# Engine orders written out by hand for a conditioned residual kernel: no loops, halved units, Newton step in PSUM, three buffers for xm and z

## What is computed

```
dg, db, ug, ub = cond @ down_gamma, cond @ down_beta, cond @ up_gamma, cond @ up_beta
down = x @ (down_project * dg + db)        # 256 -> 64, per batch
up   = relu(down) @ (up_project * ug + ub) # 64 -> 256, per batch
x2   = x + (up + x)
styles = cond @ (affine_w / sqrt(128)).T + affine_b
dcoefs = rsqrt(sum((weight * styles)**2, axis=2) + 1e-08)
y    = clip((x2 * styles) @ weight.T * dcoefs + bias, -256, 256)
out  = x2 + y
```

## Time and profile before

| | |
|---|---|
| median of three runs | 96.34 us (96.22 to 96.43) |
| span of the profiled execution, first to last instruction | 93.1 us |
| around the span (96.34 less 93.1) | 3.2 us |
| busy TensorE, VectorE, ScalarE, GpSimd | 79.1, 69.7, 56.8, 56.4 us |
| mean granted TensorE clock | 0.951 |
| moved by DMA | 9.40 MB |

### The profile page before, as it was taken

The page is one execution under the profiler, slowest core; times in us unless marked ns, Lnnn a source line. Parts: engine busy times, 40 slices in busy tenths (PEclk is TensorE's granted clock), DMA queues, the critical chain, the costliest instruction groups (busy, mean ns, idle before and its releaser), DMA issues.

```text
span 93.1 us, 1465 instructions
## 1 busy us (share of the span) xinstructions
PE 79.1 (85%) x408; PEld 49.3 (53%) x408; DVE 69.7 (75%) x113; ACT 56.8 (61%) x125; POOL 56.4 (61%) x42
## 2 busy tenths in 40 slices
PE   3985999999489937999999999999999959969340
PEld 3943497659264623356746665584665634534230
DVE  1002055579999999989997989999799999959900
ACT  6052539493920076274499389929956997993440
POOL 5900222118994997068579656857984799897000
PEclk9999589999999997599999999999999999999995
DMA  1999405160520006000057140050006000601566
GB/s 14 300 317 320 134 0 175 58 199 26 142 83 0 0 13 212 0 4 4 7 178 273 59 166 0 0 196 29 0 0 225 0 0 0 225 4 50 175 233 218
DMA packets 9861, 9.40 MB, mean 101 GB/s; under 512 B 1020, under 2 KB 9792, under 8 KB 9856
## 3 DMA queue, kind: packets, MB, share of 16 engines
q1 hardware_dynamic: 9104, 8.75, 29.0%
q10 hardware_dynamic: 576, 0.33, 1.2%
q0 software_dynamic: 176, 0.26, 1.0%
...
## 4 chain that ended last, share of the span: by engine, by line
PE 50%; DVE 23%; issue 10%; ACT 6%; DMA 5%; POOL 2%; ACTq 1%; DVEq 0%; POOLq 0%
PE ps_y L728 19%; PE ps_down L697 12%; DMA vec_rows<-in_L_cond_bias_dram 5%; ACT ps_y L290 5%; PE ps_io L664 5%; PE ps_io L739 4%; PE ps_up L711 3%; PE ps_y L697 2%; PE ps_up L712 2%; DVE ps_up L426 2%; DVE x L433 2%; DVE dm_t L386 2%; DVE z L474 2%; DVE act_hl L420 1%; DVE z L481 1%
## 5 line engine op out<-in xcount | busy, mean ns | idle before, releaser
L728 PE MATMUL ps_y<-xm,wT 128*128 128x512 f32 x56 | 27.2, 630 | 3.2 <-DVE z L474 2.1
L616 POOL TENSOR_TENSOR x<-x,off_sc 128x1024 f32 (+2 forms) x8 | 16.7, 2090 | 8.2 <-DVE x L433 8.2
L290 ACT ACTIVATE ps_y<-ps_y,vec_cols,demod 128x64 f32<-128x64 f32 x64 | 19.4, 404 | 3.2 <-PE ps_y L728 3.2
L608 POOL TENSOR_TENSOR off_sc<-act_sum,up_tab 128x1024 f32<-128x1024 f32 (+1 forms) x8 | 14.4, 1800 | 8.5 <-ACT act_sum L257 8.5
L728 PEld LDWEIGHTS ps_y<-xm,wT 128*128 128x128 f32 x56 | 10.7, 200 | 15.6 <-issue 10.6
L627 POOL TENSOR_TENSOR xm<-x,style 128x1024 f32 (+2 forms) x8 | 14.2, 1771 | 1.2 <-POOL x L616 0.8
L257 ACT ACTIVATE act_sum<-ps_sum 128x512 f32<-128x512 f32 x8 | 4.8, 598 | 13.9 <-DVE demod L398 7.0
L426 DVE TENSOR_TENSOR ps_up<-ps_up,up_tab 128x1024 f32<-128x1024 f32 x8 | 9.8, 1226 | 1.4 <-PE ps_sum L713 1.2
L433 DVE TENSOR_TENSOR x<-ps_up,x 128x1024 f32<-128x1024 f32 (+1 forms) x8 | 9.8, 1221 | 0.7
L697 PE MATMUL ps_down<-xT,dp_sb 128*64 128x256 f32 x56 | 8.2, 415 | 1.6 <-DVE act_hl L420 1.6
L261 ACT ACTIVATE out_nat<-ps_io 128x1024 f32 (+1 forms) x7 | 7.4, 1055 | 2.9 <-PE ps_io L739 2.9
...
## 6 DMA issues: line engine op xcount, KB each, us to landing
x_nat<-in_x_dram SPq DMA_DIRECT2D x7, 512.0 KB, 3.6
out_dram<-out_nat SPq DMA_DIRECT2D x7, 512.0 KB, 2.9
x_nat<-in_x_dram SPq DMA_DIRECT2D x2, 256.0 KB, 3.0
out_dram<-out_nat SPq DMA_DIRECT2D x2, 256.0 KB, 2.3
w_sb<-in_L_cond_weight_dram SPq DMA_DIRECT2D x1, 256.0 KB, 6.9
...
```

What stands on the lines that cost most here:

```text
L290: last = act.activation(tokens, tokens, ACT.Identity, bias=vec_cols[:, DC + c:DC + c + 1], scale=demod[:, c, bass.ds(t.n * TB + b, 1)])
L608: pool.tensor_tensor(by_batch(off_sc[:, 0:chunks]), sums, per_batch(up_tab[:, 1, 0:chunks, bass.ds(t.n * TB, TB)]), ALU.mult).then_inc(off ...
L616: pool.tensor_tensor(x2[:, t.n, 0:chunks], x2[:, t.n, 0:chunks], off_sc[:, 0:chunks], ALU.add).then_inc(x2_ready, 1)
L728: last = pe.matmul(y_bank(t, o), wT[:, c, o * P:(o + 1) * P], xm[:, t.parity, c], start=(i == 0), stop=(i == DC - 1))
```

## The change

Every engine's program is now a flat list. What moves in it:

- Start: `cond` is loaded from ACT's queue instead of SP's, so `down_project` and tile 1 follow tile 0 on SP directly. PE does `down(0)` ahead of the transposes of `affine_w` and of the two vectors; on POOL's queue the vectors are loaded ahead of `affine_w`. The down tables are made in one DVE copy instead of four, from `ps_up`. ACT makes the squares of the style and of the weight; POOL did.
- The tile kept in SBUF is `hT`, the plain transposed x, one buffer a tile. The second copy (`double`) is gone: x2 is kept halved. The up tables are times 0.5, the style table times 2, `demod` times 0.5, the cap is 128, and `evacuate_out` multiplies by 2.
- `x_nat` has a buffer a tile, `xm` and `z` have three, `act_sum` two. 
- Newton: the root, its argument and the product are in `ps_y[:, 0]`; only the reciprocal and `demod` are in SBUF. The step is done in one piece on DVE, ahead of `scale_down(2)`, and PE waits for it before `linear(0, 0)`, since it lies in the bank that this product writes.
- `transpose_out` comes later relative to `transpose_in` and `linear`; `linear` is at places cut between its two chunks.
- Tiles 5 and 6 are treated like all others. POOL does both chunks to the end. The last tile is cut by tokens, not features: `end_linear(part)` makes both output chunks for half of the tokens in `ps_y[:, part]`, and DVE does scale, caps and `finish` for a half (`end_scale`, `end_cap`, `end_finish`). ACT has no part in its demodulation.

```diff
-        x_nat = sb("x_nat", [P, 2, TJ, D])
-        xT = sb("xT", [P, 2, DC, T])
+        x_nat = sb("x_nat", [P, TILES, TJ, D])
+        hT = sb("hT", [P, TILES, DC, T])
-        act_sum = sb("act_sum", [P, T])
+        act_sum = sb("act_sum", [P, 2, T])
-        x2 = sb("x2", [P, TILES, DC, T])
-        xm = sb("xm", [P, 2, DC, T])
-        z = sb("z", [P, 2, DC, T])
+        xm = sb("xm", [P, 3, DC, T])
+        z = sb("z", [P, 3, DC, T])
...
+        def norm_part(i):
+            return ps_y[:, 0, i * DC * B:(i + 1) * DC * B]
+        norm_sum, norm_q, norm_root, norm_u = (norm_part(i) for i in range(4))
...
-            sp.dma_start(cond_sb[:], cond).then_inc(cond_in, 16)
...
+            act.dma_start(cond_sb[:], cond).then_inc(cond_in, 16)
...
-            def double(t):
-                act.activation(x2[:, t.n].rearrange("p c t -> p (c t)"), ps_io[:], ACT.Copy,
-                               scale=2.0).then_inc(x_doubled, 1)
...
+            def newton_step():
+                dve.wait_ge(root_done, 1)
+                dve.reciprocal(dm_r[:], norm_root).then_inc(newton, 1)
+                dve.wait_ge(newton, 1)
+                dve.tensor_tensor(norm_u, norm_q, dm_r[:], ALU.mult).then_inc(newton, 1)
+                dve.wait_ge(newton, 2)
+                dve.tensor_tensor(norm_u, norm_u, dm_r[:], ALU.mult).then_inc(newton, 1)
+                dve.wait_ge(newton, 3)
+                dve.tensor_scalar(norm_u, norm_u, -0.5, 1.5, ALU.mult, ALU.add).then_inc(newton, 1)
+                dve.wait_ge(newton, 4)
+                dve.scalar_tensor_tensor(out=demod[:].rearrange("p c b -> p (c b)"), in0=norm_u, scalar=0.5,
+                                         in1=dm_r[:], op0=ALU.mult, op1=ALU.mult).then_inc(newton, 1)
+                dve.wait_ge(newton, 5)
...
+            def end_scale(part):
+                dve.wait_ge(end_y_ps, part + 1)
+                first = LAST * TB + part * HB
+                tokens = ps_y[:, part].rearrange("p (c b s) -> p c b s", c=DC, s=S)
+                dve.tensor_tensor(tokens, tokens, per_batch(demod[:, :, first:first + HB]),
+                                  ALU.mult).then_inc(end_scaled, 1)
...
+            def end_linear(part):
+                pe.wait_ge(xm_ready, TILES)
+                pe.wait_ge(z_ready[part], LAST)
+                for o in range(DC):
+                    for c in range(DC):
+                        last = pe.matmul(ps_y[:, part, o * HT:(o + 1) * HT], wT[:, c, o * P:(o + 1) * P],
+                                         xm[:, LAST % 3, c, halves(part)], start=(c == 0), stop=(c == DC - 1))
+                last.then_inc(end_y_ps, 1)
...
+            up(1)
+            pe.wait_ge(newton, 5)
+            linear(0, 0)
+            pe.wait_ge(lo_ready, 2)
+            linear(0, 1)
+            down(3)
...
```

More of the change, by code:

```diff
@@ L12 @@
 P = 128
-Tile = namedtuple("Tile", "n parity half")
 CLAMP = 256.0
@@ L338, in _ @@
[L338 to L351 removed]
+            evacuate_sum(0)
@@ new lines, in _ @@
+            scale_up(2)
+            finish(0, 1)
+            add_up(2)
+            relu_low(3)
+            demodulate(1)
+            cap(1, 0)
+            finish(1, 0)
+            scale_down(4)
+            sum_down(4)
+            scale_up(3)
+            relu_low(4)
+            cap(1, 1)
+            add_up(3)
+            finish(1, 1)
+            scale_down(5)
+            cap(2, 0)
+            sum_down(5)
+            finish(2, 0)
+            scale_up(4)
+            demodulate(2)
@@ new lines, in _ @@
+            relu_low(5)
+            cap(2, 1)
+            add_up(4)
+            finish(2, 1)
+            scale_down(6)
+            cap(3, 0)
+            sum_down(6)
+            finish(3, 0)
+            scale_up(5)
+            demodulate(3)
+            relu_low(6)
+            cap(3, 1)
+            add_up(5)
+            finish(3, 1)
+            scale_down(7)
+            cap(4, 0)
+            sum_down(7)
+            finish(4, 0)
+            scale_up(6)
+            demodulate(4)
@@ new lines, in _ @@
+            add_up(6)
+            relu_low(7)
+            cap(4, 1)
+            finish(4, 1)
+            scale_up(7)
+            cap(5, 0)
+            finish(5, 0)
+            demodulate(5)
+            add_up(7)
+            cap(5, 1)
+            finish(5, 1)
+            cap(6, 0)
+            finish(6, 0)
+            demodulate(6)
+            cap(6, 1)
+            finish(6, 1)
+            for part in range(2):
+                end_scale(part)
+                end_cap(part)
+                end_finish(part)
```

816 lines of the change are left out of this document (337 added, 479 removed).

## The result

The changed kernel takes 88.46 us (median of four runs, 88.26 to 89.51) against 96.31 us (96.22 to 96.43) for the kernel before: a ratio of 0.9198, 95% interval 0.914 to 0.9256, 7.9 us less. The profiled execution took 88.29 us, with a span of 86.1 us and 2.2 us around it.

The account below looks back on a forecast made before the run. TensorE was taken as the bound in the middle, VectorE a near second. Span 93.1, less 6.5 gained, plus 1.3 given back, gives 87.9; with 3.2 around it, 91.2 us forecast, range 89.3 to 94.4.

Parts of the forecast that it names:

- 6.5 gained: From the beginning to the results of up(3): these come at 38.6 instead of 45.10 us.
- 1.3 given back: At the end of the kernel, where less work is shared: 1.3 us of the gain lost again.
- The start: Up to the results of up(0): through at 16.2 instead of 19.2, 3.0 us earlier, 1.7 of it the clock.
- one dip stays: Rival, chance 0.14: the start's DMA leaves TensorE half idle, one clock dip costs 1.7 us, time 92.9.
- Newton: Tile 0's second half: four small steps at 0.21 to 0.28 us each, 1.2 us instead of 4.4.
- of the 3.5 beyond the first stage 1.7 is again the clock: From up(0)'s results to up(3)'s: 3.5 us gained, 1.7 of it from the clock dip being gone.
- the sum over VectorE: Middle and end: VectorE's work from 16.2, 64.6 us, plus 1.7 of waits, gives 82.5 and a span of 86.9.
- TensorE's walk: Middle and end, walked through TensorE: waits of 0.5 to 0.9 us at three products, giving a span of 88.6.
- gains nothing by itself: ACT's saved copy, 1.02 us a tile: claimed to gain nothing by itself, since ACT waits.
- Newton as long as before: Rival, chance 0.06: Newton in PSUM is no shorter and now gates linear(0, 0), time 94.1 us.
- the late ring: Rival, chance 0.14: the add_up, POOL, linear, ACT, cap ring stalls VectorE 0.4 us in six tiles, time 93.6.
- the slower one: Rival, chance 0.09: TensorE's short waits in every tile bring repeated clock dips, 1.7 us each; four give 98.0.

Follow-up runs that it names:

- e1: The kernel before, run again unchanged: 96.56 us, against 95.30 for the kernel before on the same chip.
- e6b: The changed kernel with the old start (cond on SP's queue, affine_w loaded before the vectors, affine transposes ahead of down(0)): 91.35 us.
- e12: The changed kernel with the scaling of tile 6, channel 0, moved from ScalarE to VectorE: 87.90 us.
- e9: The changed kernel, run again unchanged: 89.34 us, against 95.77 for the kernel before on the same chip.
- e2: The kernel before with its hardware loops written out: 95.02 us, against 95.30 for the kernel before on the same chip.
- e3: The kernel before with only the start reordered (cond on ACT's queue, vectors before affine_w, down(0) before the affine transposes): 94.86 us against 95.30.
- e8b: The changed kernel with a second ScalarE copy of tiles 1 to 7 put back, into a scratch buffer: 92.12 us.
- e14: The changed kernel with the second ScalarE copy put back for tiles 2 and 3 alone: 91.84 us.
- e5b: The changed kernel with Newton's root, its argument and the product back in SBUF, same place in the queues: 90.36 us.
- e10: The changed kernel with the second ScalarE copy put back for tiles 4 to 7 alone: 88.05 us.
- e13: The changed kernel with the second ScalarE copy put back for tile 1 alone: 90.01 us.

## Why the prediction was off, point by point

**Three terms were mis-sized.** The forecast is the old span of 93.1, less 6.5 gained up to the results of `up(3)`, plus 1.3 given back behind them, plus 3.2 around the span. Measured are 7.2 gained (45.10 less 37.90), 0.2 given back (from there to the end 48.2 us instead of 48.0), and 2.2 around the span. The forecast was too long by 0.7, 1.1 and 1.0 us. (87.9 and 3.2 are 91.1; the 91.2 has 0.1 more than its terms.)

**The term around the span (1.0 us).** "With 3.2 around the span" took the difference between a median and another execution for a constant. It is 1.8 in the kernel before and 2.2 in the changed one. The step on like executions is 94.9 (the estimate in e1) to 88.3. With 2.2 the range would have begun at 88.3 and just held the result; the centre would still have been 1.6 too high.

**The start was right but for the reach of one rule.** `down(0)` at 6.5 (forecast 7.0, `down_project` landed sooner), tile 1 at 9.4 (9.2), ScalarE through with tile 1 at 12.3 (12.5), `up(0)` started at 14.6 and was through at 16.0 (16.2). The results of `up(0)` came 3.2 us earlier (forecast 3.0), 0.9 of it because the transposes of tile 2 now stand behind it. The 2.9 us of e6b are another quantity: its `up(0)` starts later than that of the kernel before (18.70 against 17.82). That a standstill of TensorE brings the dip holds only in part: behind a DMA 0.9 and 1.2 us (e12) did not and 1.8 did in e9; a gap of 2.1 us did in the kernel before and e1, and did not in e2, e3, e8b and e14. The rival "one dip stays" did not happen in the runs of the result but does happen: it is a matter of the execution.

**Newton was right in mechanism and place.** Steps of 0.30 us where 0.21 to 0.28 had been priced, the end at 22.0 (22.2), `linear(0, 0)` behind POOL at 23.30 (23.2) with TensorE not waiting for Newton. e5b prices it alone at 1.4 to 1.9 us.

**From linear(0) to up(3) the walk was 0.8 us too long.** It put gaps of TensorE of 0.2 to 0.6 us into this stretch; from 23.30 to the results of `up(3)` at 37.9 (38.6) the trace has none. And "of the 3.5 beyond the first stage 1.7 is again the clock" was priced too high: where the dip is missing in the old order (e2), it is worth 0.8. VectorE's instructions begin up to 0.1 us before the one ahead has ended where they do not depend on it, and the walk laid them end to end.

**Behind up(3) both ways of counting were too long (1.1 us), and the sum over VectorE came close by luck.** VectorE went from 16.1 to 82.1 in 65.95 us where the sum said 66.3. But 4.1 of these are waits, where the forecast found 1.7, and its own work with the small gaps is 61.9 where 64.6 stood: about 7.7 a tile, not 8.0. Two errors of 2.4 and 2.7 us cancelled. The waits of VectorE from 16.12 to 82.07, the two largest of six (in all, times, longest):
```profile
DVE ps_y L342 <- ACT ps_y L208: 1.5, 1, 1.5
DVE ps_y L336 <- PE ps_y L584: 0.8, 3, 0.5
```
From there to the end it took 4.0 instead of 4.4: 86.1 against the sum's 86.9. TensorE's walk gave 88.6: 0.7 too late at `up(3)`, and waits of 0.5 to 0.9 us at three products, of which `linear(4, 0)` has none and the other two 0.22 and 0.28 (`linear(5, 0)` and `linear(5, 1)` have 0.31 and 0.16 instead). The 87.9 was taken between the two because neither was safe; the measured span lies under both, and the choice cost 1.0 us of the 1.8 in the span.

**That the saved ACT copy "gains nothing by itself" was wrong.** It holds for tiles 4 to 7 (e10) and fails for tiles 1 to 3: 0.8 us before `up(0)` (e13) and 2.0 behind it (e14, with the copies where that kernel has them). ScalarE waits on average, but in the start it is in the chain. The error didn't reach the number, since the walk of the start had the copy out of ScalarE's way; it reached the reasons.

**The rivals.** Newton as long as before, the late ring and the slower one didn't come. The granted clock stayed at 1.00 from 16 to 82 us, with gaps of 0.2 to 1.1 us in seven places. The rule of the Trainium skill, "TensorE: Matmul & The Clock Gate", section "A second HAM failure mode: psum-queue depth-cycling", by which such gaps make the clock swing, is not borne out by this trace.

**Where the 7.9 us are.** By the profiled spans 7.0, and all of it lies ahead of the results of `up(3)`: these come 7.2 us earlier, the stretch from there to the last transposes takes 43.4 us in both kernels, and what follows 4.8 instead of 4.6. Of the 7.2, `up(0)` starts 3.2 us earlier, 2.3 for equal work (tile 2's transposes moved), which leaves 4.9 between it and `up(3)`. Taking parts back singly costs 1.4 (Newton), 2.0 (copies of tiles 2 and 3) and 1.3 (halves at the end, against whole channels, which the kernel before did not have in that form). The last of these lies behind `up(3)`, where nothing is gained in sum, so it only pays for the shared work that was given up. The first two overlap with the dip of the kernel before at 36 to 40, and how the 4.9 divide among them is not shown. Shown is that start and Newton, put on the old order, bring less than half. Not tried alone are the buffer a tile for `x_nat`, the second one for `act_sum`, and the later `transpose_out`.
